# Attention of batches 0 to 2 taken by pairs of tiles, with the low products of a pair made from 64 partitions each

## The reference, cut to what matters

```python
features_n = rmsnorm(features, fn_w)            # the 64 context rows of a batch
scores = einsum('btf,bsf->bts', Q, K) * scale   # Q from layernorm(x), K from features_n
attn = softmax(scores, axis=-1)
attended = einsum('bts,bsf->btf', attn, features_n)
x = x + tanh(g_xattn) * attended
x = x + tanh(g_ffn) * ffn(layernorm(x))         # base matmul, plus experts by gate
```

## Time and profile before

| | |
|---|---|
| median of 3 runs | 474.91 us |
| profiled execution, its own time | 474.56 us |
| its span, first to last instruction | 472.8 us |
| TensorE busy (matmuls) | 466.7 us, 99% of the span |
| weight loads busy | 399.8 us, 85% |
| VectorE busy | 357.6 us, 76% |
| ScalarE, GpSimd busy | 174.0 us, 120 us |
| mean granted clock of TensorE | 0.999 of full |

### The profile page before, as it was taken

One profiled execution on the slowest core, in us unless ns is written; L12 is line 12 of the kernel. 1 busy time (PEld: TensorE's weight loads), 2 busy tenths in 40 slices (PEclk: granted clock), 3 DMA queues, 4 the chain that ended last, 5 costly groups with the idle time before them and its releaser, 6 DMA issues.

```text
span 472.8 us, 6969 instructions
## 1 busy us (share of the span) xinstructions
PE 466.7 (99%) x2495; PEld 399.8 (85%) x2495; DVE 357.6 (76%) x746; ACT 174.0 (37%) x349; POOL 119.9 (25%) x107
## 2 busy tenths in 40 slices
PE   8999999999999999999999999999999999999996
PEld 6898999998888888888888888888888888888885
DVE  1787996598879958779977979867786677877632
ACT  4947632241224214126335525242251522315200
POOL 0020501003353343346143306040320403204000
PEclk9999999999999999999999999999999999999999
DMA  8993139958676468469479550311305041040202
GB/s 307 411 413 155 52 96 399 395 179 310 196 259 215 173 207 288 157 220 339 179 269 423 244 177 0 126 56 54 125 0 180 0 134 45 21 158 1 89 1 89
DMA packets 22114, 84.40 MB, mean 179 GB/s; under 512 B 2624, under 2 KB 3904, under 8 KB 19264
## 3 DMA queue, kind: packets, MB, share of 16 engines
q1 hardware_dynamic: 21792, 83.81, 48.7%
q10 hardware_dynamic: 288, 0.15, 0.1%
HBM read 61.93 MB, written 22.02 MB: 178 GB/s over the span
## 4 chain that ended last, share of the span: by engine, by line
PE 98%; DMA 1%; ACT 0%; DVE 0%; DVEq 0%; issue 0%
PE bank L768 11%; PE bank L772 11%; PE bank L770 11%; PE bank L645 11%; PE bank L681 7%; PE bank L683 7%; PE bank L682 7%; PE bank L741 5%; PE bank L526 4%; PE bank L743 2%; PE bank L667 2%; PE bank L666 2%; PE bank L668 2%; PE bank L720 2%; PE bank L721 2%; PE bank L787 2%
## 5 line engine op out<-in xcount | busy, mean ns | idle before, releaser
L1551 POOL TENSOR_TENSOR small<-small,tiny 128x1 f32<-128x1 f32 (+2 forms) x25 | 21.7, 867 | 164.4 <-DVE small L1182 138.1
L1531 DVE SCALAR_TENSOR_TENSOR xs<-bank,tiny,xs 128x512 f32<-128x512 f32 (+1 forms) x61 | 43.3, 738 | 21.8 <-PE bank L772 16.0
L681 PE MATMUL bank<-xth,gram 128*128 128x512 f32 x144 | 57.3, 398 | 0.0
L683 PE MATMUL bank<-xtl,gram 128*128 128x512 f32 x144 | 56.3, 391 | 0.0
L682 PE MATMUL bank<-xth,gram 128*128 128x512 f32 x144 | 56.1, 390 | 0.0
L768 PE MATMUL bank<-wh_B,zh 128*128 128x512 f32 x116 | 47.0, 405 | 0.0
L768 PE MATMUL bank<-wh_T,zh 128*128 128x512 f32 (+1 forms) x116 | 46.6, 402 | 0.0
L1579 POOL TENSOR_TENSOR sq_sum<-sq_sum,sq 128x512 f32<-128x512 f32 x24 | 32.0, 1335 | 56.5 <-DVE sq L1361 56.5
L772 PE MATMUL bank<-wh_B,zl 128*128 128x512 f32 x116 | 45.6, 393 | 0.0
L770 PE MATMUL bank<-wl_B,zh 128*128 128x512 f32 x116 | 45.4, 391 | 0.0
L772 PE MATMUL bank<-wh_T,zl 128*128 128x512 f32 (+1 forms) x116 | 44.7, 386 | 0.0
(11 more groups left out here) (199 smaller groups left out, 1130.9 us busy)
## 6 DMA issues: line engine op xcount, KB each, us to landing
xst<-x_dram SPq DMA_DIRECT2D x16, 512.0 KB, 4.1
xz<-xt_dram SPq DMA_DIRECT2D x16, 512.0 KB, 7.4
out_dram<-xs SPq DMA_DIRECT2D x14, 512.0 KB, 2.7
xa<-x_dram SPq DMA_DIRECT2D x12, 512.0 KB, 3.4
x<-xa SPq DMA_DIRECT2D x12, 512.0 KB, 2.9
xs<-x SPq DMA_DIRECT2D x12, 512.0 KB, 4.1
wq_raw<-wq_dram SPq DMA_DIRECT2D x8, 512.0 KB, 13.7
t_raw_T<-wb_dram SPq DMA_DIRECT2D x4, 1024.0 KB, 15.6
```

The costliest lines, as they stand in the source:

```text
L681: pe.matmul(acc[:, :], gram[:, g, 0, :], xth[b % 2][:, r, :], start=r == ROWS[j][0], stop=False)
L683: done = pe.matmul(acc[:, :], gram[:, g, 0, :], xtl[b % 2][:, r, :], start=False, stop=r == ROWS[j][-1])
L1531: dve.scalar_tensor_tensor(out=xs[slot][:, cols], in0=bank[n_bank][:, 0:hi - lo], scalar=tg[:, 1:2], in1=xs[slot][:, cols], op0=ALU.mult, ...
```

## The change

1. Stage `attend2` takes the place of `attend` for the 12 tiles of batches 0 to 2. It handles a pair q of tiles and one half h of the columns: `pt` by `fnh` for both tiles (as before, over 128 partitions), and then two low products, of 64 partitions each: for the even tile partitions 0 to 63, for the odd tile 64 to 127. Each goes to its own bank. The term low share x low row is no longer part of the sum.
2. `px` is laid out so that the high shares of an odd tile stand in columns 64 to 127: two copies and two subtractions where there were one and one.
3. `xa` is one tensor of both tiles; loads and stores move one half of the columns of two tiles (pieces of 2 KB where there were 4 KB). The load for half 1 of the next batch stands behind `load_xt` (batch 1) or behind the three `w_load` and the first `y` (batch 3), no longer ahead of them.
4. `load_xs` waits for both halves' stores; for the first two places in `xa` also for the last ones.
5. `IDLE` is 5.

```diff
-        IDLE = 4
+        IDLE = 5
...
+                if b == B - 1 and j == 0:
+                    first.append(("load_xa", (B - 2) * TPB // 2, 1))
...
-                        t = (b - 1) * TPB + j - 4
-                        first += [("attend", t), ("x1", t)] + [("load_xa", t + 2)] * (t + 2 < NT - TPB)
+                        q, h = (b - 1) * TPB // 2 + (j - 4) // 2, (j - 4) % 2
+                        first += [("attend2", q, h), ("x1", q, h)] + [("load_xa", q + 1, h)] * (q + 1 < (NT - TPB) // 2 and j + 1 < FB)
...
                 first.append(("load_xt", b + 2))
+            if 0 < b < B - 2:
+                first.append(("load_xa", b * TPB // 2, 1))
...
+                elif stage == "attend2":
+                    q, h = i
+                    b, cols = 2 * q // TPB, half(h)
+                    accs = []
+                    for c in range(2):
+                        acc = ring_open((stage, q, h, c), "dve")
...
+                        pe.matmul(acc[:, :], pt[b // 3][:, 2 * q % TPB + c, :], fnh[:, cols], start=True, stop=False)
+                        accs.append(acc)
+                    for c, acc in enumerate(accs):
+                        rows = slice(c * S, c * S + S)
+                        pe.matmul(acc[:, :], pt[b // 3][rows, 2 * q % TPB + c, :], fnl[rows, cols], start=False,
+                                  stop=True).then_inc(p_ring, 1)
...
+            def two_tiles(rows, q, h):
+                return rows[2 * q * P:(2 * q + 2) * P, half(h)].rearrange("(c p) d -> p c d", c=2)
...
+                        sp.wait_ge(st_xa[h], 16 * q)
+                    sp.dma_start(xa[:, :, half(h)], two_tiles(x, q, h)).then_inc(ld_xa[h], 16)
...
-                        sp.wait_ge(st_xa[3 - slot], 16 * (NT - TPB) // NXA)
+                        for h in range(NH):
+                            sp.wait_ge(st_xa[h], 16 * (NT - TPB) // 2)
...
-                    dve.tensor_copy(px[:, :, 0:S], pexp[:, :, :]).then_inc(v_pxh, 1)
-                    dve.wait_ge(v_pxh, b + 1)
-                    dve.tensor_tensor(px[:, :, S:P], pexp[:, :, :], px[:, :, 0:S].bitcast(F32),
-                                      ALU.subtract).then_inc(v_px, 1)
+                    for c in range(2):
+                        dve.tensor_copy(px[:, c:TPB:2, c * S:c * S + S], pexp[:, c:TPB:2, :]).then_inc(v_pxh, 1)
+                    for c in range(2):
+                        dve.wait_ge(v_pxh, 2 * b + c + 1)
+                        dve.tensor_tensor(px[:, c:TPB:2, S - c * S:P - c * S], pexp[:, c:TPB:2, :],
+                                          px[:, c:TPB:2, c * S:c * S + S].bitcast(F32), ALU.subtract).then_inc(v_px, 1)
```

More of the change, by code:

```diff
@@ L154, in build @@
         fn_raw = at("fn_raw", [P, D], F32, r_fr)
-        xa = [at(f"xa{i}", [P, D], F32, r_xa + i * ROW) for i in range(NXA)]
+        xa = at("xa", [P, 2, D], F32, r_xa)
         xs = [at(f"xs{i}", [P, D], F32, o) for i, o in enumerate((r_kt + 2 * ROW, r_kt + 3 * ROW, r_xa + ROW, r_xa))]
@@ L268, in build @@
         ld_x = [sem(f"ld_x{i}") for i in range(NXA)]
-        ld_xa = [sem(f"ld_xa{i}") for i in range(NXA)]
-        st_xa = [sem(f"st_xa{i}") for i in range(NXA)]
+        ld_xa = [sem(f"ld_xa{h}") for h in range(NH)]
+        st_xa = [sem(f"st_xa{h}") for h in range(NH)]
         ld_xs = [sem(f"ld_xs{i}") for i in range(4)]
@@ L399, in build @@
                     first += [("x_stat", t) for t in {2: [8], 3: [9], 4: [10], 5: [11], 6: [12], 7: [13]}.get(j, [])]
-                    first += {4: [("load_fn", 0)], 6: [("load_xa", 0), ("load_xa", 1)], 7: [("load_bb",)]}.get(j, [])
+                    first += {4: [("load_fn", 0)], 6: [("load_xa", 0, 0), ("load_xa", 0, 1)], 7: [("load_bb",)]}.get(j, [])
                 if b == 1 and 1 < j < 4:
@@ L709, in tensor @@
                     transposes(acc, st_sb[:, :].rearrange("p (j t) -> p j t", j=TPB))
+                elif stage == "attend2":
[4 more added lines that the diff above has]
+                        acc = ring_open((stage, q, h, c), "dve")
+                        if (2 * q) % TPB == 0 and h == c == 0:
+                            engine, count = ring.empty(ring.number["pt", b])
+                            pe.wait_ge(ring_sem[engine], count)
+                            pe.wait_ge(v_fn, b + 1)
+                        pe.matmul(acc[:, :], pt[b // 3][:, 2 * q % TPB + c, :], fnh[:, cols], start=True, stop=False)
[4 more added lines that the diff above has]
+                                  stop=True).then_inc(p_ring, 1)
                 elif stage == "attend":
@@ L916, in sync @@
                     if t < NT - TPB:
-                        sp.wait_ge(st_xa[t % NXA], 16 * (t // NXA + 1))
+                        for h in range(NH):
+                            sp.wait_ge(st_xa[h], 16 * (p + 1))
                         src = x1_dram.ap()
@@ L1093, in scalar @@
                     if 0 < b < B - 1:
-                        act.wait_ge(p_ring, ring.full(("attend", b * TPB - 1, 1)))
+                        act.wait_ge(p_ring, ring.full(("attend2", b * TPB // 2 - 1, 1, 1)))
                     act.activation(pt[b // 3][:, :, :], four((stage, b)), ACT.Copy).then_inc(ring_sem["act"], 1)
@@ L1450, in vector @@
                                           hw[h][:, :, 0:HEAD].bitcast(F32), ALU.subtract).then_inc(v_hw, 1)
+                elif stage == "attend2":
+                    q, h = i
+                    dve.wait_ge(ld_xa[h], 16 * (q + 1))
+                    for c in range(2):
+                        n = ring.number[stage, q, h, c]
+                        dve.wait_ge(p_ring, n + 1)
+                        dve.scalar_tensor_tensor(out=xa[:, c, half(h)], in0=bank[T_BANKS[n % 2]][:, :],
+                                                 scalar=rt[:, 2 * q + c:2 * q + c + 1], in1=xa[:, c, half(h)], op0=ALU.mult,
+                                                 op1=ALU.add).then_inc(ring_sem["dve"], 1)
                 elif stage == "attend":
```

30 lines of the change are left out of this document (12 added, 18 removed).

## The result

The changed kernel takes **478.48 us** (median of 12 runs, 477.43 to 479.79), the kernel before in the same session 475.69 us (12 runs). The ratio is 1.005, 95% interval 1.0036 to 1.0064: slower by 1.7 to 3.0 us. The forecast was 476.8 us, with 472.0 to 477.6 as the range: the sign is right, the size is not, and the time lies outside the range.

What follows compares the result with a forecast made beforehand. The prediction took TensorE's own line as the bound. The low pairs' +1.9 us, all other terms zero, on a base of 474.91 us gave 476.8 us, with a range of 472.0 to 477.6.

Steps and rivals of the forecast that it cites:

- (1): Low products of 12 attention stages: running side by side saves 0.22 us, two shape changes cost 0.38; +1.9 us in all.
- (5): DVE's sums: the first of a stage can begin about 0.2 us later, TensorE waiting only at `tops`; zero.
- (3): Loads of `xz` and `xa`: `xz` goes some 2.5 us sooner, `xa` moves in half-size pieces; zero.
- A: Rival for the low products: no price for the change of shape, each stage saves 0.22 us; 472.3 us, chance 0.32.
- B: Rival for the low products: half the price of the shape change, so no difference; 474.6 us, chance 0.13.
- C: Rival for the low products: full price and no sharing, +4.6 us; 479.5 us, chance 0.05.
- (2): Split of the shares in `px`: the chain ends 0 to 0.3 us later, within 0.29 us of cover; zero.
- (6): Fifth product of zeros at the start: ends at 5.44, before the first real matmul at 5.50; zero.
- (4): `load_xs` waiting for both stores: lands at 246.8, DVE reads it at 247.28, half a microsecond of cover; zero.
- the sign that I gave: Trace sign for the loads: `DVE xz` should have no wait left on the DMA, where it had 1.78 us.
- my signs: Trace signs, among them that new TensorE waits on DVE or DMAs, at `px` or tile 3, would mean wrong in kind.
- D: The forecast itself, full price with sharing in the low products: 476.8 us, own range 476.0 to 477.8, chance 0.50.

Runs made afterwards that it cites:

- f3: The changed kernel with low products over all 128 partitions and the load of B22 ahead of `load_xs`; 474.6 us, ratio 0.9965 to before.
- g3: The kernel of f3 once more, in another session; 475.33 us, ratio 0.9969 to before.
- h3: The changed kernel with low products over all 128 partitions, B22 still behind `load_xs`; 476.76 us.
- h4: The kernel of f3 again, as a corner of the two by two table; 475.60 us, ratio 0.9972 to before.
- e4: The changed kernel with the load of B22 ahead of `load_xs`, low products still in pairs; 476.89 us, ratio 1.0005 to before.
- f1: The kernel before, unchanged, run again; 476.91 us, ratio 1.0011 to its own runs.
- g2: The kernel of h4 with four products of zeros instead of five; 475.25 us, ratio 0.9973 to before.
- f4: The changed kernel with B22 first and the high products also on 64 partitions, leaving out the low shares; 477.11 us, ratio 1.0023 to before.
- h2: The kernel of e4 again, as a corner of the two by two table; 477.46 us.
- g4: The kernel before with the second `xa` load of a batch held back, so the last batch's `xz` is issued sooner; 476.05 us, ratio 0.9981.
- h1: The changed kernel itself, as a corner of the two by two table; 478.53 us.
- f2: The changed kernel, unchanged, run again; 478.31 us, ratio 1.0044 to before.
- g1: The kernel of h4 with the `xa` load not held back, so `xz` stands behind it; 480.09 us, ratio 1.0058 to before.

## Why the prediction was wrong

**Right: the mechanism of (1) and its size.** The products run side by side, the shape change costs its 0.19 us twice, and the stage loses. Forecast +1.9 us for the pair, measured +1.8. The price of emptying came from `k_norm`, where the columns are halved, and holds for rows; that of the open load came from `k01`. Two things in it were off and cancelled, so the closeness of 1.9 and 1.8 is partly luck: a stage with what follows it loses 0.22 us in batches 1 and 2 and about 0.1 in the last, where I had put 0.16 everywhere; and the kernel without pairs itself waits longer at `tops`, by 0.3 to 0.5 us, so the sum on TensorE (2.3 us) is more than the difference in time (1.8). That the sum at `tops` comes later was term (5), which I had bounded by 2 x 0.2 and set to zero; it measures 2 x 0.11. The rest, up to 0.25 us, is a load of x that lands later, of the kind that (3) had put at zero (f3, g3, h3; h4 has none of it). Rivals A, B and C are out: the price is there (A), in full (B), and so is the sharing (C).

**Right: (2) and (6), zero.** From the start of `rt` to the end of the last piece of `px`, the split chain takes 0.894 us in e4 (146.098 to 146.992) and the old one 0.884 (146.043 to 146.927): 0.01 us. The waits for `px` that some executions show have another cause, `xz`, and appear in the kernel before with its unsplit chain too (f1). g2 shows the same within 0.1 us with four products of zeros.

**Wrong: (4) `load_xs`, "Zero".** This is the step that failed: +1.1 us. The reader that I named is not what was late in the changed kernel (it started at 250.65 and did not wait; in f4 it did, 2.07 us). What I left out is the queue: B22, behind both loads, is issued 3.9 us later, of which TensorE was late itself by 3.3, and so only 0.6 us late against TensorE's own line. It also takes longer, 7.7 us from issue to landing where it took 5.8; with B22 first it is 5.9 to 6.0 (e4, h2, h4), so both parts come with its place in the queue. That makes B22 2.4 us late against TensorE's own line, and the chain from it did not have so much cover.

**Wrong: (3) the loads, "Zero".** It was zero in the execution that I read. In the second one (f1) the wait for `xz` reaches TensorE, and issuing it sooner removes that: about -0.9 us by g4, whose interval also holds zero, and -1.3 to -1.7 us by f3, g3 and h4, which hold this part and nothing else that was found to gain. That it is the whole of their lead is argued, not shown. "Pieces of half the size could at worst double" the time of a transfer was more than needed for the form (the page has 4.3 us for a load of `xa` where it had 3.4), but the store with a load close in front went from 2.7 to 5.7 and 6.8 us, and I asked only who reads the load behind it, not what else stands behind that store on the queue. Of the sign that I gave, no wait of DVE for this `xz`, 0 to 0.84 us were left (h1, e4).

**Wrong: the base.** I set the sum on three runs around 474.91 and a profiled execution of 474.56. The lowest of over a hundred runs of this kernel is 474.51, and its medians in the five sessions are 475.69, 476.69, 476.12, 476.87 and 477.39. I had read an execution in which every load came in time. The changed kernel is at 478.48, 478.31 and 478.53 in three of these sessions, so the difference is 2.8, 2.2 and 1.1 us. By parts: +1.8 for the pair, +1.1 for B22, -0.9 to -1.7 for `xz`; the sum is 1.2 to 2.0 us. The forecast of +1.9 lies within it by two errors of opposite sign, which is luck. The time missed the forecast by 1.7 us in the first session: 0.8 of that is the base and 1.1 is B22, less what `xz` gives back, and the rest is open. Loads that land late in one execution and not in the next are of that size: in the profiled execution of 478.22 us they make 1.35 of the 4.60 us (0.74 at 97 to 101, 0.24 at 147, 0.37 at 314), in f2's of 477.35 us 0.4. I had also not named the place where TensorE's new waits stand, `mt` and line 788, among my signs, and the ends of my own range for D (476.0 to 477.8) are a little wider than the 0.06 us per stage that I gave for them.

**A version that beats both.** The change with full low products and with B22 ahead of `load_xs` (f3, g3, h4) is faster than before by 0.28% to 0.35% in three sessions, and than the changed kernel by 2.9 us in one (475.60 against 478.53).

## What to carry to other kernels

Two half arrays side by side save one product (0.22 us here), and going into that shape and out of it costs nearly two (0.38): price the change of shape before anything else. Several pairs of one shape behind each other pay it once, but in f4 two pairs brought TensorE's line only 0.04 us per stage below before, and the time did not follow. When a transfer on a queue gains a wait, list what is queued behind it and follow each of them to TensorE, not only the reader of the transfer itself. And a cover that one profiled execution shows as just enough is not cover: take a second execution, and look at which waits come and go, before a term is set to zero.

## What the runs showed that I had not expected

- The first product behind a change of shape keeps its price for one step more: starts at 153.35 and 153.69, 0.34 us apart, though the load of the second stands 0.11 us behind the start of the first.
- A stall of TensorE of 4.0 us ended in a granted clock of 0.50, the level of 1.2 GHz, over the stretch from 188 to 192 us, and the clock took 2.6 us more than the stall (g1).
- A store of 512 KB took 2.6 to 2.8 us with no load of x under way, in rows of 4 KB or of 2 KB, and 4.8 to 5.3 us with a load of 512 KB issued 0.4 us ahead of it, again in both forms (before and g1). In g1 three stores in a row took 3.7, 4.7 and 6.8 us, with the load 1.5, 0.8 and 0.5 us ahead: each long store held back the next load, which then stood closer to the next store.
- The kernel before varies from 474.51 to 480.75 us in 138 runs, the changed one from 477.27 to 480.1 in 35 and 483.02 in one more. That the load of `xz` without slack makes the wider spread would fit, but is not shown: g4, which issues it sooner, still goes from 474.62 to 478.79.
